# Output projection on high and low parts: nine f32r matmuls in place of three fp32 ones

## What is computed

```python
q = heads(hidden_states @ W_q)
probs_t = jax.nn.softmax(scores_t, axis=-1)
text_out = einsum(probs_t, heads(text_ehs @ W_v))
qsem = _l2norm(einsum(probs_t, text_ehs))
fused = attn_scores + SEM_SCALE * (qsem . ip_n)
probs_ip = jax.nn.softmax(fused, axis=-1) * spatial_mask
out = text_out + einsum(probs_ip, v_ip)
out = out @ W_out + b_out + residual
```

## Time and profile before

| | |
|---|---|
| median of 3 runs | 413.31 us (412.75 to 413.77) |
| the profiled execution | 411.41 us |
| its span, first to last instruction | 409.6 us |
| granted TensorE clock, mean | 0.997 |
| TensorE matmuls busy | 393.6 us (96%) |
| TensorE weight loads busy | 319.5 us (78%) |
| VectorE busy | 220.2 us (54%) |
| ScalarE busy | 206.0 us (50%) |
| GpSimd busy | 206.3 us (50%) |

### The profile page before, as it was taken

The page is one execution under the profiler, slowest core; times in us unless marked ns, Lnnn a source line. Parts: engine busy times, 40 slices in busy tenths (PEclk is TensorE's granted clock), DMA queues, the critical chain, the costliest instruction groups (busy, mean ns, idle before and its releaser), DMA issues.

```text
span 409.6 us, 9494 instructions
## 1 busy us (share of the span) xinstructions
PE 393.6 (96%) x3653; PEld 319.5 (78%) x3653; DVE 220.2 (54%) x482; ACT 206.0 (50%) x484; POOL 206.3 (50%) x218
## 2 busy tenths in 40 slices
PE   7999799899899999999999999999999999999995
PEld 4648688678788878888789878887888878876762
DVE  0795764575267534665366526663556646643432
ACT  1534134555645565555556564456455366458722
POOL 3020361262527872576437662687247443844981
PEclk9999999999999999999999999999999999999998
DMA  8499994338204802273207511470208210001000
GB/s 259 140 292 234 213 172 84 92 126 166 75 2 150 145 14 72 75 161 61 82 6 193 97 49 36 146 144 18 72 2 168 51 40 2 3 3 39 3 16 15
DMA packets 29455, 38.03 MB, mean 93 GB/s; under 512 B 14361, under 2 KB 26745, under 8 KB 28729
## 3 DMA queue, kind: packets, MB, share of 16 engines
q1 hardware_dynamic: 28514, 36.36, 37.0%
q10 hardware_dynamic: 896, 1.07, 0.9%
HBM read 28.50 MB, written 8.81 MB: 91 GB/s over the span
## 4 chain that ended last, share of the span: by engine, by line
PE 88%; DVE 3%; ACT 2%; issue 2%; DMA 2%; POOL 1%; POOLq 0%; SPq 0%; ACTq 0%; DVEq 0%
PE PR L905 42%; PE Y L905 27%; PE P L905 10%; PE O L905 8%; DMA pb<-wq 1%; DVE big L773 1%; PE PR L1063 1%; ACT big L681 1%; ACT er L685 1%; POOL pb L547 1%; DVE mx L807 1%; DMA qst<-ma 0%; POOLq L169 0%; SPq L460 0%; ACT cTs L729 0%
## 5 line engine op out<-in xcount | busy, mean ns | idle before, releaser
L547 POOL TENSOR_TENSOR pb<-pb 128x448 f32<-128x448 f32 x78 | 89.1, 1142 | 110.4 <-DVE pb L829 104.9
L807 DVE TENSOR_REDUCE mx<-PR 112x1 f32<-112x371 f32 x160 | 83.7, 540 | 78.1 <-PE PR L905 77.1
L905 PE MATMUL Y<-er,Gh 128*128 128x448 f32 x240 | 95.3, 397 | 1.7 <-ACT er L685 0.8
L829 DVE TENSOR_TENSOR pb<-big,Y 128x448 f32<-128x448 f32 x120 | 72.6, 621 | 39.2 <-PE Y L905 39.0
L905 PE MATMUL Y<-er,Gl 128*128 128x448 f32 x240 | 87.3, 364 | 0.0
L681 ACT ACTIVATE big<-P 128x448 f32<-128x448 f32 x120 | 65.2, 543 | 18.7 <-PE P L905 17.9
L685 ACT ACTIVATE er<-big 128x448 fp32r<-128x448 f32 x120 | 69.3, 578 | 3.8
L905 PEld LDWEIGHTS Y<-er,Gh 128*128 128x128 f32 x240 | 45.1, 188 | 13.7 <-DVE pb L829 9.1
L905 PE MATMUL PR<-kst,qst 96*112 96x371 bf16 x160 | 51.3, 331 | 2.2 <-DVE mx L807 2.0
L905 PEld LDWEIGHTS Y<-er,Gl 128*128 128x128 f32 x240 | 45.2, 188 | 2.1
L905 PE MATMUL P<-qst,kst 99*128 99x112 bf16 x480 | 42.0, 214 | 1.5 <-ACT big L681 1.1
(11 more groups left out here) (154 smaller groups left out, 653.5 us busy)
## 6 DMA issues: line engine op xcount, KB each, us to landing
et<-ctxT SPq DMA_DIRECT2D x8, 752.0 KB, 4.4
kst<-kd SPq DMA_DIRECT2D x7, 720.0 KB, 7.2
kd<-ks SPq DMA_DIRECT2D x16, 288.0 KB, 2.9
qst<-qd SPq DMA_DIRECT2D x48, 70.0 KB, 2.4
kst<-kd SPq DMA_DIRECT2D x7, 480.0 KB, 9.9
kst<-kd SPq DMA_DIRECT2D x9, 240.0 KB, 9.0
qd<-kst SPq DMA_DIRECT2D x4, 336.0 KB, 5.6
vx<-xr SPq DMA_DIRECT2D x8, 140.0 KB, 2.2
```

What stands on the lines that cost most here:

```text
L547: pool.tensor_tensor(total, total, (pz, pm)[j], ALU.add).then_inc(s_S, 1)
L807: dve.tensor_reduce(mx[b % 2][:, h:h + 1], bank[0:S, 0:T], AX.X, ALU.max).then_inc(s_free[seq[u] % NR], 1)
L829: dve.tensor_tensor((pz, pm, pa[g % 2])[j], eb[g % 3][:, 448 * j:448 * j + 448], Y[y % 2][:, 0:448], ALU.mult).then_inc(s_P, 1)
L905: return pe.matmul(o, st, mv, start=start, stop=stop, **kw)
```

## The change

`cTs` becomes a pair of f32r tensors, `cTh` (the value rounded to f32r, written by ScalarE from PSUM) and `cTl` (what is left, PSUM minus `cTh`, written by VectorE). The output weights likewise become `woh` and `wol`. Each fp32 product turns into three f32r products: high x high, high x low weights, low x high. The bank of `cT` is now freed by VectorE behind its second subtraction, and not by ScalarE. The same is done with `vrT` (`vrTh`, `vrTl`), whose low part VectorE makes in the unit `vW`, and with the pieces of image 7. The product of `pTs` with `vrWo` stays fp32.

A new unit `wo` at the end of round 1 of image 0 makes `woh` on ScalarE and `wol` on GpSimd. To make room, the raw weights are loaded into a part of `kst[2]`, so the load of image 2's keys waits for `wol` too, `sq` lies in `OT[1]`, and `vrTh`, `vrTl` lie in `eh[0]`, `el[0]`.

```diff
+         "S0 m g m S1 K2 m S2 v m m wo",
...
+            if b == 0:
+                unit.update({"wo": ("wo",)})
...
+        woh = sb("woh", [128, 3, C], f32r)
+        wol = sb("wol", [128, 3, C], f32r)
...
+        cTh = sb("cTh", [128, 3, S], f32r)
+        cTl = sb("cTl", [128, 3, S], f32r)
...
                     if b == 2:
                         sp.wait_ge(s_pa, len(posp))
+                        sp.wait_ge(s_wol, 1)
...
+                if u == ("wo",):
+                    pool.wait_ge(s_woh, 2)
+                    pool.tensor_tensor(wol[:, 0:2, :], wo_s[:, 0:2, :], woh[:, 0:2, :].bitcast(f32), ALU.subtract)
+                    pool.tensor_tensor(wol[0:64, 2, :], wo_s[0:64, 2, :], woh[0:64, 2, :].bitcast(f32), ALU.subtract).then_inc(s_wol, 1)
...
+                if u == ("wo",):
+                    act.wait_ge(s_w2, 16 * REST)
+                    act.activation(woh[:, 0:2, :], wo_s[:, 0:2, :], ACT.Copy).then_inc(s_woh, 1)
+                    act.activation(woh[0:64, 2, :], wo_s[0:64, 2, :], ACT.Copy).then_inc(s_woh, 1)
...
                 elif k == "cT":
                     filled(act, u)
-                    act.activation(cTs[:, 0:2, :], bank[:, 0:2 * S].rearrange("p (c s) -> p c s", c=2), ACT.Copy)
-                    act.activation(cTs[0:64, 2, :], bank[0:64, 2 * S:3 * S], ACT.Copy).then_inc(s_free[seq[u] % NR], 1)
+                    act.activation(cTh[:, 0:2, :], bank[:, 0:2 * S].rearrange("p (c s) -> p c s", c=2), ACT.Copy)
+                    act.activation(cTh[0:64, 2, :], bank[0:64, 2 * S:3 * S], ACT.Copy).then_inc(s_cTh, 1)
...
+                elif k == "cT":
+                    b = u[1]
+                    dve.wait_ge(s_cTh, b + 1)
+                    if b < B - 1:
+                        dve.tensor_tensor(cTl[:, 0:2, :], bank[:, 0:2 * S].rearrange("p (c s) -> p c s", c=2),
+                                          cTh[:, 0:2, :].bitcast(f32), ALU.subtract)
+                    else:
+                        dve.tensor_tensor(cTl[:, 1, :], bank[:, S:2 * S], cTh[:, 1, :].bitcast(f32), ALU.subtract)
+                    dve.tensor_tensor(cTl[0:64, 2, :], bank[0:64, 2 * S:3 * S], cTh[0:64, 2, :].bitcast(f32),
+                                      ALU.subtract).then_inc(s_free[seq[u] % NR], 1)
+                elif k == "cT0":
+                    dve.wait_ge(s_ca, 1)
+                    dve.tensor_tensor(cTl[:, 0, :], Y[0][:, 0:S], cTh[:, 0, :].bitcast(f32), ALU.subtract).then_inc(s_cd, 1)
+                elif k == "vW":
+                    dve.wait_ge(s_va, 1)
+                    for c, w in enumerate(CW):
+                        last = dve.tensor_tensor(vrTl[0:w, c, :], P[1][0:w, 80 * c:80 * c + 80], vrTh[0:w, c, :].bitcast(f32),
+                                                 ALU.subtract)
+                    last.then_inc(s_vd, 1)
...
                     freed(pe, seq[("cT", b)])
-                    for c in range(3):
-                        last = mm(bank[0:S, 0:C], cTs[0:CW[c], c, :], wo_s[0:CW[c], c, :], c == 0, c == 2)
+                    for c, w in enumerate(CW):
+                        mm(bank[0:S, 0:C], cTh[0:w, c, :], woh[0:w, c, :], c == 0, False)
+                        mm(bank[0:S, 0:C], cTh[0:w, c, :], wol[0:w, c, :], False, False)
+                        last = mm(bank[0:S, 0:C], cTl[0:w, c, :], woh[0:w, c, :], False, c == 2)
```

More of the change, by code:

```diff
@@ L186, in build @@
         wvl = sb("wvl", [128, 4, C], f32r)
-        wo_s = sb("wo_s", [128, 3, C])
+        woh = sb("woh", [128, 3, C], f32r)
+        wol = sb("wol", [128, 3, C], f32r)
         Gh = [sb(f"Gh{i}", [128, 768], f32r) for i in range(2)]
@@ L198, in build @@
         Sip = sb("Sip", [S, B, H * NIP])
-        sq = sb("sq", [128, 4, B * NIP])
         nip = sb("nip", [S, B * NIP])
@@ L223, in build @@
         pTs = sb("pTs", [H * NIP, S])
-        cTs = sb("cTs", [128, 3, S])
+        cTh = sb("cTh", [128, 3, S], f32r)
+        cTl = sb("cTl", [128, 3, S], f32r)
         res = [sb(f"res{i}", [S, C]) for i in range(2)]
-        vrT = et[:, 0, 0:H * NIP * 3].rearrange("p (c n) -> p c n", c=3)
+        vrTh, vrTl = [w[:, 0, 0:H * NIP * 3].rearrange("p (c n) -> p c n", c=3) for w in (eh[0], el[0])]
         vrWo = et[0:H * NIP, 1, 0:C]
@@ L240, in build @@
         qT = kst[2][:, :, :].rearrange("p h t -> p (h t)").bitcast(f32)[:, 0:2688].rearrange("p (c n) -> p c n", c=3)
+        wo_s = kst[2][:, :, :].rearrange("p h t -> p (h t)").bitcast(f32)[:, 2688:2688 + 3 * C].rearrange("p (c n) -> p c n", c=3)
+        sq = OT[1][:, :, :].rearrange("p g s -> p (g s)")[:, 0:4 * B * NIP].rearrange("p (c n) -> p c n", c=4)
         wkip_s = big[:, 2688:2688 + 1280].rearrange("p (c n) -> p c n", c=4)
@@ L314, in build @@
         s_cTs = sem("s_cTs")
+        s_woh = sem("s_woh")
+        s_wol = sem("s_wol")
+        s_vd = sem("s_vd")
+        s_cd = sem("s_cd")
+        s_cTh = sem("s_cTh")
         s_vp = sem("s_vp")
@@ L617, in _ @@
                 bank = PR[seq[u] % NR] if k in RING else None
-                if u == ("w", 0):
+                if u == ("wo",):
+                    act.wait_ge(s_w2, 16 * REST)
+                    act.activation(woh[:, 0:2, :], wo_s[:, 0:2, :], ACT.Copy).then_inc(s_woh, 1)
+                    act.activation(woh[0:64, 2, :], wo_s[0:64, 2, :], ACT.Copy).then_inc(s_woh, 1)
+                elif u == ("w", 0):
                     act.wait_ge(s_wk, 16)
@@ L707, in _ @@
                     act.wait_ge(s_vp, 1)
-                    filled(act, ("K", u[1], 2))
-                    act.wait_ge(s_el, 2 * B)
+                    filled(act, ("V", u[1], 2))
                     for c, w in enumerate(CW):
-                        last = act.activation(vrT[0:w, c, :], P[1][0:w, 80 * c:80 * c + 80], ACT.Copy)
+                        last = act.activation(vrTh[0:w, c, :], P[1][0:w, 80 * c:80 * c + 80], ACT.Copy)
                     last.then_inc(s_va, 1)
@@ L714, in _ @@
                     act.wait_ge(s_vp, 2)
+                    filled(act, ("K", u[1], 2))
+                    act.wait_ge(s_el, 2 * B)
                     act.activation(vrWo, P[0][0:80, 0:C], ACT.Copy).then_inc(s_va, 1)
@@ L720, in _ @@
                     act.wait_ge(s_cp, 1)
-                    act.activation(cTs[:, 0, :], Y[0][:, 0:S], ACT.Copy).then_inc(s_ca, 1)
+                    act.activation(cTh[:, 0, :], Y[0][:, 0:S], ACT.Copy).then_inc(s_ca, 1)
                 elif k == "cT" and u[1] == B - 1:
                     filled(act, u)
-                    act.activation(cTs[:, 1, :], bank[:, S:2 * S], ACT.Copy)
-                    act.activation(cTs[0:64, 2, :], bank[0:64, 2 * S:3 * S], ACT.Copy).then_inc(s_free[seq[u] % NR], 1)
+                    act.activation(cTh[:, 1, :], bank[:, S:2 * S], ACT.Copy)
+                    act.activation(cTh[0:64, 2, :], bank[0:64, 2 * S:3 * S], ACT.Copy).then_inc(s_cTh, 1)
                 elif k == "cT":
                     filled(act, u)
-                    act.activation(cTs[:, 0:2, :], bank[:, 0:2 * S].rearrange("p (c s) -> p c s", c=2), ACT.Copy)
-                    act.activation(cTs[0:64, 2, :], bank[0:64, 2 * S:3 * S], ACT.Copy).then_inc(s_free[seq[u] % NR], 1)
+                    act.activation(cTh[:, 0:2, :], bank[:, 0:2 * S].rearrange("p (c s) -> p c s", c=2), ACT.Copy)
+                    act.activation(cTh[0:64, 2, :], bank[0:64, 2 * S:3 * S], ACT.Copy).then_inc(s_cTh, 1)
         @block.vector
@@ L1101, in _ @@
                     b = u[1]
-                    pe.wait_ge(s_va, 1)
+                    pe.wait_ge(s_vd, 1)
                     for c in ((0, 1), (2,))[u[2]]:
-                        last = mm(P[0][0:80, 0:C], vrT[0:CW[c], c, :], wo_s[0:CW[c], c, :], c == 0, c == 2)
+                        w = CW[c]
+                        mm(P[0][0:80, 0:C], vrTh[0:w, c, :], woh[0:w, c, :], c == 0, False)
+                        mm(P[0][0:80, 0:C], vrTh[0:w, c, :], wol[0:w, c, :], False, False)
+                        last = mm(P[0][0:80, 0:C], vrTl[0:w, c, :], woh[0:w, c, :], False, c == 2)
                     if u[2]:
@@ L1111, in _ @@
                         freed(pe, n - NR)
-                        pe.wait_ge(s_ca, 1)
+                        pe.wait_ge(s_cd, 1)
                     else:
@@ L1115, in _ @@
                     for c in ((0,), (1, 2))[part]:
-                        mm(PR[n % NR][0:S, 0:C], cTs[0:CW[c], c, :], wo_s[0:CW[c], c, :], c == 0, False)
+                        w = CW[c]
+                        mm(PR[n % NR][0:S, 0:C], cTh[0:w, c, :], woh[0:w, c, :], c == 0, False)
+                        mm(PR[n % NR][0:S, 0:C], cTh[0:w, c, :], wol[0:w, c, :], False, False)
+                        mm(PR[n % NR][0:S, 0:C], cTl[0:w, c, :], woh[0:w, c, :], False, False)
                 elif k == "o" and u[1] == B - 1:
@@ L1124, in _ @@
                     if b == 0:
-                        pe.wait_ge(s_w2, 16 * REST)
+                        pe.wait_ge(s_wol, 1)
                     freed(pe, seq[("cT", b)])
```

(6 more changed lines are left out.)

## The result

The changed kernel took 415.29 us (median of 7 runs, 414.26 to 417.13), the kernel before 413.76 us in 7 runs beside it. The ratio is 1.0049, 95% interval 1.0027 to 1.0071: slower by half a percent. A ratio here rests on all runs of both kernels and not on the two medians, whose quotient is 1.0037. In the profiled executions the span grew by 2.5 us, from 409.6 to 412.1.

What follows compares the result with a forecast made beforehand. TensorE, 88% of the chain that ended last, was taken to bound the kernel. Six `o` +0.2, image 6 0, weights 0 and tail +0.75 gave +0.95 us on 413.31, so 414.3 us; range 412.8 to 416.2.

Steps and rivals of the forecast that it cites:

- slower by over 0.3%: Whole kernel: outcome that the change lengthens the time by more than 0.3% (1.24 us); chance 0.40.
- within: Whole kernel: outcome that the time stays inside 0.3% (1.24 us) of the kernel before; chance 0.53.
- The matmuls of an `o`: TensorE, images 0 to 5: nine f32r matmuls take 1.40 us instead of 1.95 for three fp32, gaining 0.55 each.
- both extras: TensorE's nine matmuls: low end of the gain, 0.50 us, with the extra start costs 0.08 and 0.105 us.
- The wait in front: Before `o`, images 0 to 5: VectorE's two subtractions take 0.57 us and free the bank 0.59 us later each.
- The tail's order: Last stretch: VectorE's subtractions delay short steps, +0.4 us by the exponential, +0.35 before `end` 0; sum +0.75 us.
- `o` of image 6: TensorE near the end: starts 0.42 us late but is 0.5 us shorter, so about 0.
- The weights: End of round 1: ScalarE's copies, about 1.15 us, fit into 1.96 us of idle, GpSimd's subtractions delay little; cost 0.
- (a): Rival at `o`: TensorE's waiting time is given back at a later wait, so the gain stays; 410.2 us, chance 0.07.
- (b): Rival: all terms at their good ends, `o` gaining up to 0.15 us, tail costing 0.2; 412.6 to 413.3, chance 0.13.
- (d): Rival at the six `o`: VectorE's subtractions wait for GpSimd's running additions, 0.7 us on average; 418.5 us, chance 0.05.
- (c): Rival at the six `o`: VectorE's pair is dearer, 0.85 us, partly from 64 rows behind 128; 416.0 us, chance 0.13.

Runs made afterwards that it cites:

- experiment 4: Changed kernel with the third piece of `o` of images 0 to 6 run on 128 rows, 64 of them zero: 413.97 us, 1.0016 of the kernel before.
- experiment 1: Kernel before, fp32 matmuls kept, with VectorE's two subtractions added behind ScalarE's copies for images 0 to 6: 417.00 us, 1.0082 of the kernel before.
- experiment 5: Changed kernel with only VectorE's queue reordered, tail subtractions moved behind `pw'`, `r2'` and `end` 0: 416.12 us, 1.0058 of the kernel before.
- experiment 7: Kernel before, fp32 matmuls kept, with the third piece of `o` of images 0 to 6 on 128 rows, 64 zero: 411.98 us, ratio 0.9962.
- experiments 3: Changed kernel with the `cTh` products of `o` first and the `cTl` products last, images 0 to 6: 413.32 us, 0.9994 of the kernel before.

## Why the prediction was right

The time, 415.29 us, lies in the range, 1 us over the forecast. The mechanism came as forecast: the matmuls gain, the new step in front of them costs more than that, and the tail pays for VectorE's order. Of the three outcomes, though, "slower by over 0.3%", which had 0.40, is what happened by the ratio, and not "within", which had 0.53. The term that moved it across is one of the sum, and one of the signs by which the prediction called itself wrong came true: the nine matmuls take more than 1.6 us. That the time is only 1 us off is partly luck. The stretches grew by 2.65 us where 0.95 were forecast; the median rose by 1.5.

- **The matmuls of an `o`: mis-sized.** Forecast 9 x 0.145 + 0.09 = 1.40 us, gain 0.55; measured 1.65 us, gain 0.30. The step that failed is the transfer from the value projection, whose twelve matmuls keep one number of rows, to an `o` whose third piece has 64. That piece makes three spacings 0.09 us wider, and experiment 4, which takes them away, finds 1.38, close to the forecast 1.40. Over six images this is 6 x 0.25 = 1.5 us, nearly all of the difference between the +0.2 forecast and the +1.84 measured. The measured gain of 0.30 lies outside the ends 0.50 and 0.65; the lower one, meant to hold "both extras" (0.08 and 0.105), would have been 1.95 - 9 x 0.145 - 0.185 = 0.46 by its own numbers, still far off. I had the 64 rows in view only as a doubt about VectorE's pair.
- **The wait in front: right.** The pair was to take 0.57 us and takes 0.56; TensorE's start moved by 0.60 us against 0.59, and by 0.60 in experiment 1. The straight line through VectorE's neighbours gave 0.38 and 0.27, the trace has 0.39 and 0.26. The table of the Trainium skill (VectorE: DVE Perf Modes, the TRN2 errata) would have given 0.36 and 0.24, a little low; the same page's formula for an fp32 `tensor_tensor` add, (N + 151)/0.96 ns, gives, as an estimate, 0.39 for 224 elements and 0.27 for 112. That page of the Trainium skill gives it as measured at 512 and 2048 elements; here it fits the wide subtraction better than the table does, and the narrow one (64 rows, 0.26) about as well.
- **The tail's order: right in its parts.** Forecast +0.75; from the total of 0.81, less 0.17 for the `o` of image 6, 0.64 are shown by experiment 5 to be VectorE's order. The two pieces are the ones forecast: the exponential in front of the last copy of `O` (0.27 us; 0.4 forecast), and `cTl` of `cT0` in front of `end` 0 (0.33 us; 0.35 forecast). That `o` of image 6 would cost nothing was short by 0.2 us for the same reason as above, and these 0.2 us make up for the exponential, which was forecast 0.13 too high: that the total, 0.81, comes so near to 0.75 is luck in part. `end` 0 starts 0.60 us later, counted from the last `pv`, where 0.75 were named as the sign.
- **The weights: right.** ScalarE's two copies (0.73 and 0.46 us) stood ahead of an exponential, which came 0.6 us later than before, and the idle stretch behind it took that up: 1.33 us of idle are left of 1.96. TensorE runs there 0.11 us earlier than in the kernel before, ahead of the copies as behind them, so it lost nothing. GpSimd's subtractions ended at 91.84, and the keys of image 2 were issued at 93.64 as before. The timeline of the changed kernel, ScalarE's rows first, then GpSimd's and its queue's:

```profile
87.05 0.73 ACT L635 ACTIVATE woh<-kst 128x640 fp32r<-128x640 f32 x1
87.68 0.46 ACT L636 ACTIVATE woh<-kst 64x320 fp32r<-64x320 f32 x1
...
90.51 0.54 ACT L700 ACTIVATE big<-P 128x448 f32<-128x448 f32 x1 [1.33 <-PE P L944]
...
89.46 1.55 POOL L537 TENSOR_TENSOR wol<-kst,woh 128x640 fp32r<-128x640 f32 x1
90.97 0.87 POOL L538 TENSOR_TENSOR wol<-kst,woh 64x320 fp32r<-64x320 f32 x1
...
93.64 0.29 SPq L460 DMA_DIRECT2D kst<-krow  x1
```

- **The rivals.** (a), gain kept, fell: experiment 1 shows that the wait is paid in full. (b), all terms at their good ends, fell with the 0.30 us that an `o` gains. (d), a VectorE blocked by GpSimd, fell: at images 0 to 3 the wide subtraction ran beside two of GpSimd's additions, at image 6 beside none, and all seven took 391 or 392 ns, so the trace agrees with the rule of the Trainium skill (SBUF — State Buffer, Who interferes with whom) here. The row with all `cTl` subtractions of 224 elements (ns, min/median/max):

```profile
L913 DVE TENSOR_TENSOR cTl<-PR,cTh x7: 391/392/392, 150.9 to 395.5; 128x224 fp32r<-128x224 f32 x7
```

(c) named the right place (the third piece's 64 rows) on the wrong engine: VectorE's pair overlaps like the pair in the earlier trace rows (the second starts 0.09 us before the first ends), while TensorE's stream of matmuls is slowed there.

- **From the profile to the median.** The stretches say +2.65 us, the profiled execution +2.85, the medians +1.5, the ratio +2.0 with an interval of about 1.1 to 2.9. I had carried the 1.9 us between the profiled execution and the median over unchanged; in the changed kernel the profiled execution lies 1.0 us under its median. What sets this difference in single runs was not looked into beyond the clock of the first 148 us.

## What to carry to other kernels

When an operand is split for cheaper matmuls, look at who makes the low part and where TensorE stands then: products that don't need it go first. A piece with few rows can cost more than a full one with zeros, which a look at the spacings around its two borders tells. Before comparing the ends of two executions, look at the granted clock there: in experiment 7 it hid a third of the gain. A helper engine that is half idle is no free place: its queue runs in order, and a step with a late input delays the short steps behind it.

## What was not expected of the hardware

TensorE, for matmuls of 320 columns: at each change between 128 and 64 rows, in either direction, the two spacings that follow are 0.24 us instead of 0.145 (f32r), and the one from 64 to the 99 rows of the next unit is 0.24 as well; from 128 to 99 rows it is 0.15, like the spacing inside. In fp32, where a matmul has two records, the three spacings of the same places are 0.36 us instead of 0.27. Putting the third piece on 128 rows took 0.27 us off an `o`, in both types.

The loads of the weights go with it: inside a group a load starts with the matmul before its own, at such a change 0.24 us behind it. From 128 to 99 rows the load is late too, but by 0.15 us only, no more than the usual spacing, and costs nothing. That the time is tied to the change of rows is shown by experiments 3, 4 and 7; why the load can't start earlier there isn't shown by any run.
